# Reordering a five-engine software pipeline: a third buffer for the residual's x, and every engine's calls in another order

## What is computed

```python
def cross_attention(q, k, v):                    # q = layernorm(x), k = v = ctx_1024
    gi = concatenate([q, k, v], -1)              # 8 heads of 64
    ig, fg = gi @ igate_w.T + igate_b, gi @ fgate_w.T + fgate_b
    cs = cumsum(log_sigmoid(fg))
    log_D = where(tril, cs_i - cs_j, -inf) + ig_j
    m = max(log_D, -1)
    C = (q @ k.T / sqrt(64)) * exp(log_D - m)
    n = maximum(abs(C.sum(-1)), exp(-m))
    h = (C / (n + 1e-6)) @ v
    return layernorm_by_head(h) * out_w

x = x + cross_attention(layernorm(x), ctx, ctx)
x = x + fp8_ffn(layernorm(x))                    # one 512 x 512 matmul, quantised input and kernel
```

## Time and profile before

| | us |
|---|---|
| median of 3 runs | 1698.84 |
| lowest and highest | 1691.91, 1705.91 |
| profiled execution | 1687.96 |
| its span in the profile | 1686.2 |

### The profile page before, as it was taken

How to read it: one execution, slowest core, us unless ns; L and a number is a source line. 1 busy time by engine, 2 the same in 40 slices (tenths; PEclk the granted TensorE clock), 3 DMA queues, 4 the chain that set the end, 5 groups by cost and what they waited for, 6 DMA issues and landing times.

```text
span 1686.2 us, 79011 instructions
## 1 busy us (share of the span) xinstructions
PE 1487.8 (88%) x31104; PEld 1046.6 (62%) x31104; DVE 1491.5 (88%) x4091; ACT 1319.7 (78%) x3206; POOL 1208.2 (72%) x1101
## 2 busy tenths in 40 slices
PE   1589998999999999899999899998999999999884
PEld 0366666666666666666666666666666666666662
DVE  5669999899989999989999899998999989998894
ACT  4568887888888888878888788887888878888662
POOL 2047777778777777867777777777777777777884
PEclk9789999999999999999999999999999999999996
DMA  5468888888888888877887878888788888887552
GB/s 182 135 197 250 261 257 246 247 250 257 260 242 267 253 257 245 265 239 241 261 251 257 251 238 253 264 254 257 245 250 260 263 251 245 270 253 233 192 170 82
DMA packets 138523, 402.61 MB, mean 239 GB/s; under 512 B 26216, under 2 KB 36456, under 8 KB 138152
## 3 DMA queue, kind: packets, MB, share of 16 engines
q1 hardware_dynamic: 138152, 397.52, 77.4%
HBM read 325.23 MB, written 72.22 MB: 236 GB/s over the span
## 4 chain that ended last, share of the span: by engine, by line
PE 31%; DVE 28%; DMA 19%; issue 13%; ACT 6%; POOL 3%; DVEq 1%; SPq 0%; ACTq 0%; POOLq 0%
DMA o_sb<-in_x 10%; PE work L555 7%; DMA out<-o_sb 5%; DVE o_sb L1076 5%; PE y L594 5%; DVE bn L1036 5%; DVE dec L982 4%; PE qk L523 4%; PE turn L451 4%; DMA x_sb<-in_x 3%; DVE bn L958 2%; PE turn L462 2%; POOL x L1234 2%; DVE carry L989 2%; DVE bn_h L1019 2%
## 5 line engine op out<-in xcount | busy, mean ns | idle before, releaser
L1216 POOL TENSOR_TENSOR x<-x,h_r 128x512 f32<-128x512 f32 x256 | 294.8, 1152 | 131.4 <-DVE x L1028 91.3
L1229 POOL TENSOR_TENSOR x<-x,w_out 128x512 f32<-128x512 f32 x256 | 358.1, 1399 | 17.7
L1234 POOL TENSOR_TENSOR x<-x,o_sb 128x512 f32<-128x512 f32 x256 | 321.4, 1277 | 52.9 <-DMA o_sb<-in_x 52.3
L555 PEld LDWEIGHTS work<-c_first,dec 128*64 128x64 f32 x4096 | 259.4, 138 | 93.6 <-issue 92.5
L555 PE MATMUL work<-c_first,dec 128*64 128x65 f32 x4096 | 291.1, 224 | 20.4 <-DVE carry L989 16.8
L555 PE MATMUL work<-c_sb,dec 128*64 128x65 f32 x4096 | 294.0, 225 | 0.0
L523 PE MATMUL qk<-qT,kT 64*64 64x128 f32 (+1 forms) x8192 | 238.5, 251 | 59.9 <-DVE dec L982 44.2
L594 PE MATMUL y<-w_ffn,zq 128*128 128x512 bf16 x1024 | 268.4, 385 | 2.2 <-issue 2.2
L523 PEld LDWEIGHTS qk<-qT,kT 64*64 64x64 f32 x8192 | 200.6, 134 | 100.4 <-issue 76.0
L555 PEld LDWEIGHTS work<-c_sb,dec 128*64 128x64 f32 x4096 | 259.2, 138 | 0.2 <-issue 0.2
L674 ACT ACTIVATE dec<-arg 128x384 f32<-128x384 f32 x512 | 243.0, 475 | 7.3 <-PE arg L505 6.1
(11 more groups left out here) (113 smaller groups left out, 3229.0 us busy)
## 6 DMA issues: line engine op xcount, KB each, us to landing
c_sb<-in_ctx SPq DMA_DIRECT2D x128, 520.0 KB, 7.2
x_sb<-in_x SPq DMA_DIRECT2D x128, 512.0 KB, 5.5
kT<-in_keys SPq DMA_DIRECT2D x128, 512.0 KB, 7.2
o_sb<-in_x SPq DMA_DIRECT2D x128, 512.0 KB, 5.2
out<-o_sb SPq DMA_DIRECT2D x128, 512.0 KB, 3.0
c_first<-in_ctx SPq DMA_DIRECT2D x256, 130.0 KB, 5.9
arg_queries<-query_parts SPq DMA_DIRECT2D x128, 144.0 KB
arg_keys<-key_parts SPq DMA_DIRECT2D x128, 12.0 KB
```

What stands on the lines that cost most here:

```text
L555: last = mm(work_ps[rows, u, c * W:(c + 1) * W], heads_dec[:, slot * Q:(slot + 1) * Q], src, start=True, stop=True)
L1216: pl.tensor_tensor(h, h, h_r[:, t * NH:(t + 1) * NH].unsqueeze(2).broadcast_to([P, NH, DH]), ALU.mult).then_inc(h_normed[t].sem, 1)
L1229: pl.tensor_tensor(h, h, w_out[:, :], ALU.mult).then_inc(h_scaled[t].sem, 1)
L1234: pl.tensor_tensor(x1[:, b.k % 2, t, :], x1[:, b.k % 2, t, :], o_sb[:, b.k % 2, t, :], ALU.add).then_inc(x1_set[t].sem, 1)
```

## The change

Three buffers for o_sb, FIRST = -13, and another order of calls in the slot of each engine. In SP's slot the batches of the loads change too (x: m + 12 for m + 10, keys: m + 9 for m + 7, parts and first: m + 2 for m + 1, store_parts: m + 3 for m + 2, own: m for m - 2). In functions nothing changes but the index of o_sb and the two waits for it. The diff, cut where lines are only the new index:

```diff
-FIRST, LAST = -12, 4
+FIRST, LAST = -13, 4
+OWN_RING = 3
-        o_sb = sb("o_sb", [P, 2, T, F])
+        o_sb = sb("o_sb", [P, OWN_RING, T, F])
...
@@ SP @@
             def load_own(b):
-                if b.follows(2):
-                    sp.wait_ge(stored, b.count(16, -16))
-                sp.dma_start(o_sb[:, b.k % 2, :, :], rows_of(x, b)).then_inc(own_in[b.k % 2], 16)
+                if b.follows(OWN_RING):
+                    sp.wait_ge(stored, b.count(16, 16 - 16 * OWN_RING))
+                sp.dma_start(o_sb[:, b.k % OWN_RING, :, :], rows_of(x, b)).then_inc(own_in[b.k % OWN_RING], 16)
...
-                if live(m + 10):
-                    load_x(m + 10)
-                if live(m + 1):
-                    load_parts(m + 1)
-                if live(m - 2):
-                    load_own(m - 2)
-                if live(m + 7):
-                    load_keys(m + 7)
-                if live(m + 1):
-                    load_first(m + 1)
                 if live(m + 3):
                     load_c(m + 3)
-                if scans(m + 2):
-                    store_parts(m + 2)
+                if live(m + 2):
+                    load_parts(m + 2)
                 if live(m - 3):
                     store(m - 3)
+                if live(m + 9):
+                    load_keys(m + 9)
+                if live(m + 2):
+                    load_first(m + 2)
+                if scans(m + 3):
+                    store_parts(m + 3)
+                if live(m + 12):
+                    load_x(m + 12)
+                if live(m):
+                    load_own(m)
@@ PE @@
-                if live(m + 3):
-                    arg(m + 3, 0)
                 if live(m + 9):
                     turn_round(m + 9, 1)
...
                 if live(m + 3):
                     states(m + 3)
+                if live(m + 4):
+                    arg(m + 4, 0)
```

More of the change, by code:

```diff
@@ L389, in store @@
                 sp.wait_ge(*out_set[1].of(b))
-                sp.dma_start(rows_of(out, b), o_sb[:, b.k % 2, :, :]).then_inc(stored, 16)
+                sp.dma_start(rows_of(out, b), o_sb[:, b.k % OWN_RING, :, :]).then_inc(stored, 16)
             sp.dma_start(w_gates[:, :, :, :], gate_w).then_inc(gate_w_in, 16)
@@ L822, in slot @@
                     part_constants()
-                if live(m - 2):
-                    quantise(m - 2)
                 if live(m + 1):
                     decay(m + 1, 3)
+                if scans(m + 2):
+                    scan_exps(m + 2)
+                if scans(m + 4):
+                    scan_abs(m + 4)
                 if scans(m + 3):
                     parts_middle(m + 3)
[L829 to L833, removed]
                 if live(m):
                     normaliser_square(m)
+                if scans(m + 4):
+                    scan_exp(m + 4)
                 if live(m + 8):
                     keep_turned(m + 8, 0)
-                if scans(m + 2):
-                    scan_exps(m + 2)
+                if live(m + 10):
+                    x_logs(m + 10)
+                if scans(m + 4):
+                    scan_relu(m + 4)
+                if live(m + 1):
+                    keep_state(m + 1)
+                if scans(m + 4):
+                    scan_log(m + 4)
+                if live(m + 10):
+                    x_rstds(m + 10)
+                if live(m + 2):
+                    decay(m + 2, 0)
+                if live(m + 9):
+                    norm_apply(m + 9, 0)
                 if live(m):
                     head_log(m)
+                if live(m + 9):
+                    norm_apply(m + 9, 1)
+                if live(m):
+                    head_rstd(m)
                 if live(m + 1):
[L843 to L847, removed]
+                    keep_heads(m + 1)
                 if live(m + 8):
                     keep_turned(m + 8, 1)
[L850 to L855, removed]
                 if live(m - 1):
@@ L1120, in slot @@
                     ffn_weights(m.k - WEIGHTS_AT)
+                if live(m - 4) and wide_z:
+                    quantise_wide(m - 4)
+                if live(m - 4):
+                    finish(m - 4, 0)
                 if live(m - 1):
@@ L1130, in slot @@
                     mix_stats(m - 3, 1)
+                if live(m + 9):
+                    norm_moments(m + 9)
+                if live(m - 3):
                     mix_moments(m - 3)
@@ L1133, in slot @@
                     head_centre(m - 2, 0)
-                if live(m + 9):
-                    norm_moments(m + 9)
+                if scans(m + 2):
+                    scan_sums(m + 2)
+                if scans(m + 1):
+                    scan_exponents(m + 1)
                 if live(m - 3):
@@ L1154, in slot @@
                     normaliser_clip(m - 1)
-                if live(m + 10):
-                    norm_stats(m + 10, 0)
-                if live(m - 1):
+                    head_stats(m - 1, 0)
                     head_stats(m - 1, 1)
[L1159 to L1166, removed]
             slots_by_range(dve, slot)
@@ L1254, in slot @@
                 if live(m + 8):
-                    residual(m + 8, 0)
+                    residual(m + 8, 1)
+                if live(m + 11):
+                    weigh_keys(m + 11)
+                if live(m + 9):
+                    head_norm(m + 9, 0)
+                    head_norm(m + 9, 1)
+                    scale_heads(m + 9, 0)
+                if scans(m + 13):
+                    scan_rest(m + 13)
+                if live(m + 9):
+                    scale_heads(m + 9, 1)
             slots(slot)
```

36 lines of the change are left out of this document (13 added, 23 removed).

## The result

The changed kernel takes 1832.4 us (median of 4, 1818.9 to 1838.7) against 1697.1 for the kernel before: a ratio of 1.078, interval 1.071 to 1.086. The forecast was 1646, so the sign was wrong.

What follows compares the result with a forecast made beforehand. Bound: PE, DVE and the DMA system within 15% of the period, waits losing 59 us. Gain 45, less 9 for parts, plus 4 in the drain: 46 off the profile's 1687.96, 1642; as median 1646, range 1602 to 1690.

Steps and rivals of the forecast that it cites:

- the sign: Whole kernel: faster, 1646 us forecast; chance 0.85 of faster by over 1%, 0.07 of slower.
- x and keys: SP's queue: loads go out for later batches, SP stands at load_keys; DVE's 18.1 us of waits for x mostly go.
- the 9 us for the parts: Scan parts' image, issued behind x, own and c: PE waits 0.3 us per group, 9 us in all.
- Third o_sb buffer: Residual's x buffer: load_own waits for store(b-3), not store(b-2), and is issued earlier; gains its share of 59 us.
- 59 us can be had. I take three quarters (45): Steady slots: waits that come and go lose 2.05 us per group over 29 groups; 45 of 59 us recovered.
- the o_sb loop: Store, load_own, residual and next store of one buffer: 23.61 us for two batches, 11.8 per batch, as long as the engine schedule.
- The rival "slower": Parts image behind other transfers in SP's queue lands 4 us late, PE's arg waits: 57 us more, 1755; chance 0.07.
- DVE's reordering worth 0, 18 to either side: DVE's slots: scan_sums joins the slot of scan_a and scan_max, 12.54 to 13.15 us; another slot gains 0.6; net 0.
- keep_turned hidden behind `across`: ACT's copy of 0.6 us, now behind keep_heads, covered by PE's `across` of 0.70: cost nothing, at most 77 us.
- head_log and head_var moved at no cost: ACT's head_log behind keep_state and decay, POOL's head_var behind the residual: cost 0; POOL's worst case 37 us.
- A full DMA system would move about 251/0.83 = 302 GB/s: DMA engines in the steady part: full rate from share and throughput, making a batch of 3.15 MB take 10.4 us.
- 4 us off the drain: Batches 119 to 127, at 10 to 11 us a slot, said to be bound by the o_sb loop: 4 us gained.

Runs made afterwards that it cites:

- the fastest kernel: Changed kernel with SP's list of before, but load_own(m - 1) and load_x(m + 11); three o_sb buffers and new DVE, ACT, POOL order kept: 1643.0 us, ratio 0.973 to the kernel before.
- x alone: Kernel before with load_x(m + 11) for load_x(m + 10) and nothing else, two o_sb buffers: 1688.6 us, ratio 0.9995.
- two pairs: New against old DVE, ACT, POOL order, three buffers: paced SP slot, 1713.2 against 1728.3; SP's list of before with load_own(m - 1), load_x(m + 11), 1643.0 against 1658.5.
- a third: New against old order of DVE, ACT and POOL, both with SP's list of before and three o_sb buffers: 1748.6 against 1724.2 us.
- in a fourth: New against old order of DVE, ACT and POOL, both with SP's new slot and three o_sb buffers: 1832.4 against 1828.0 us.

## Why the prediction was wrong

By its own steps:

- *x and keys: "the SP queue first stands at load_keys" and "Everything behind" it "moves with it".* This is the larger step that failed: SP's new slot was costed at nothing but the 9 us for the parts. It costs 84 us (1832.4 against 1748.6 with SP's list put back), and with the three buffers and the old engine orders it makes the whole loss (1828.0). The stand was seen; it was 6.9 us in the mean of 120 where the prediction had some 5. But only the landing of each load against its own reader was checked. Reader by reader that was nearly right: DVE's waits for x fell to 0.6 us, POOL's for o_sb to 1.9 (200 to 1500 us), and only the parts image was late. The reader left out was PE's own program: 124.7 us of bare waits where there were 26.5, and 45 us of matmuls at the lower clock.
- *Third o_sb buffer: "Gain: its share of the 59 us. No instruction is added; the number of DMAs is the same."* This step failed too, by its sign: 29 us lost with the buffer alone (1724.2), 61 with a fourth in the fastest kernel. It took the wait of load_own for the store as pure cost. The same wait also splits SP's stream of loads, and PE's bare waits double and more where it goes (26.5 to 53.9 and to 68.3).
- *"59 us can be had. I take three quarters (45)".* The fastest kernel takes 1643.0, 11.96 us a slot; the prediction said 1646 and a mean near 12.0. That supports the account of the schedule, but the nearness is in part luck: that kernel has another list of SP, and its gain is made up of 34 us for own and x and 15 for the engines' order, where the prediction had it from the o_sb loop and x, and 0 from the engines. x alone gave nothing.
- *The rival "slower"* named the same burst ("denser than any now") and the wrong victim, the parts image: 8.3 us of waits between 200 and 1500 us, 11.0 in all, where the prediction took 9. Its condition was a lateness of 4 us once per group; what came was 1.7 us in the mean at 72 of 187 borders of PE's program. A hint was there: DMA at 0.83, and 38.8 us of PE waits with "issue" as releaser in the kernel before.
- *DVE's reordering worth 0, 18 to either side.* It depends on the loads: 15 us faster in two pairs, 24 us slower in a third, 4 us slower (within the noise) in a fourth. The slots were attributed badly: between two `carried`, scan_sums stays in the same slot, so the slot with the two other scans did not grow (shortest 12.69 in the changed kernel and 12.47 in the fastest, against 13.15 expected). And the 16.9 us in which DVE waits for its own bn_stats were called out of reach of any reordering; they are gone in the fastest kernel, since another call now stands between the two.
- *keep_turned hidden behind `across`; head_log and head_var moved at no cost.* Held: no such wait shows in the fastest kernel.
- *"A full DMA system would move about 251/0.83 = 302 GB/s".* The row 807:808 above has 365 GB/s at a share of 0.99, so the 10.4 us per batch is an estimate on the long side.
- *4 us off the drain, "where the o_sb loop of 11.8 binds".* Slots of 10 to 11 us cannot be bound by a loop of 11.8. From `carried` of batch 119 to the end it took 121.8 us before, 125.1 in the changed kernel and 121.8 in the fastest.

## What to carry to other kernels

A kernel whose PE executes tens of thousands of small matmuls, as this one, has one more load on its DMA engines: its program. Before taking any wait of the load queue away, look at PE's waits whose releaser is "issue", and check whether they lie at equal distances in the instruction count; here the DMA engines were busy 0.83 and a deeper ring made the kernel slower by this alone. Move loads earlier, but keep a wait in the queue that splits the burst.

## What the runs showed of the hardware

- PE's program arrives in pieces of 16.4 KB, 256 of its instructions, of which about 250 are matmuls and weight loads. At 72 of 187 borders PE stood, up to 4.1 us, and each time went on 2.2 to 2.9 us after the start of a packet of its program.
- These packets start late when the DMA engines are full of data: more than 5 us after PE has entered the piece before at 24 borders, with data at 0.95 of the engines in between; 4 times in the kernel before.
- Of 27 such stops of 2 us and more, 19 were followed by some 3 us at the lower clock level (granted 0.50), in which the four ffn matmuls took 1.91 us instead of 1.03. Over the span PE was busy 45 us longer.
- About 1 us more or less between the store and the next load of x moved the kernel by 29 us (2.97 to 2.15 us, two to three buffers) and by 61 us (3.25 to 2.16, three to four).
- Open: why the order of the changed kernel makes packets late so much oftener. Both kernels issue a batch in 5.5 to 5.6 us, so the bytes issued at once are not the whole rule.
